# Combined rows gated on VectorE in halves, Silu in the routed experts, scaling behind a split, rows normalized in halves

## The reference

```python
x = L0_attn_x
xn = _layernorm(x)
s = sigmoid attention of xn (q, k layer-normed; scores - log S), projected, * layerscale
g = _silu(_L0_ffn_ref(xn, ...))     # 16 routed experts (top 4) + a shared expert: silu(x @ gate) * (x @ up) @ down
x = x + s * g
xn = _layernorm(x)
s = _L1_attn_ref(xn, k, v)          # a bank of 2048 keys: gelu(scores / norm * sqrt(n)) @ v
g = _silu(_L1_ffn_ref(xn, ...))     # ternary weights: gelu(xn @ W1 + b1) @ W2 + b2
x = x + s * g
```

## Time and profile before

| what | us |
|---|---|
| median of 3 runs (1235.54 to 1235.79) | 1235.58 |
| the profiled execution, time | 1233.56 |
| the profiled execution, span | 1231.8 |
| DVE busy | 875.9 (71%) |
| ACT busy | 553.7 (45%) |
| POOL busy | 423.0 (34%) |
| second attention with its projection | about 525 to 741 |
| routed experts | about 324 to 525 |
| ff stage | about 749 to 890 |

### The profile page before, as it was taken

One profiled execution on the slowest core, in us unless ns is written; L12 is line 12 of the kernel. 1 busy time (PEld: TensorE's weight loads), 2 busy tenths in 40 slices (PEclk: granted clock), 3 DMA queues, 4 the chain that ended last, 5 costly groups with the idle time before them and its releaser, 6 DMA issues.

```text
span 1231.8 us, 26611 instructions
## 1 busy us (share of the span) xinstructions
PE 1195.6 (97%) x8888; PEld 851.7 (69%) x8889; DVE 875.9 (71%) x1893; ACT 553.7 (45%) x1050; POOL 423.0 (34%) x376
## 2 busy tenths in 40 slices
PE   5899999999999999999999999999999999999998
PEld 4556566676688888866666667767766666666665
DVE  8697965556668766678889889998765545555554
ACT  6545632333366666665343345666542222222221
POOL 3353777776036460056777742212000000000000
PEclk8999999999999999999999999999999999999999
DMA  9488355553297665522566647541211011101100
GB/s 300 169 336 319 117 172 167 166 187 134 72 290 229 202 193 188 165 82 76 151 208 196 192 137 241 162 138 37 68 52 52 18 35 52 52 0 51 52 18 18
DMA packets 137830, 169.14 MB, mean 137 GB/s; under 512 B 12899, under 2 KB 126710, under 8 KB 135446
## 3 DMA queue, kind: packets, MB, share of 16 engines
q1 hardware_dynamic: 114438, 125.49, 31.2%
q0 software_dynamic: 12368, 33.70, 8.6%
q10 hardware_dynamic: 10944, 8.92, 2.3%
HBM read 84.18 MB, written 83.89 MB: 136 GB/s over the span
## 4 chain that ended last, share of the span: by engine, by line
PE 75%; DVE 14%; issue 6%; ACT 3%; DVEq 1%; DMA 1%; SPq 0%; ACTq 0%
PE bank L1219 25%; PE sums L1275 15%; PE sums L1234 11%; PE bank L1138 7%; PE sums L1148 4%; PE bank L1080 3%; PE bank L1118 3%; DVE reg_w L2162 2%; DVE stat L1880 2%; PE sums L1090 1%; PE sums L1071 1%; DVE reg_e L2152 1%; DVE reg_qk L1835 1%; DVE reg_w L1835 1%; PE bank L1183 1%
## 5 line engine op out<-in xcount | busy, mean ns | idle before, releaser
L2162 DVE TENSOR_SCALAR reg_w<-reg_w 128x512 f16<-128x512 f32 x320 | 148.4, 464 | 200.3 <-ACT reg_w L1659 199.7
L1835 DVE SCALAR_TENSOR_TENSOR reg_w<-reg_w 128x512 f16<-128x512 f32 x320 | 222.7, 696 | 11.0
L1234 PE MATMUL sums<-reg_v,reg_w 128*128 128x256 f16 x1536 | 188.1, 273 | 1.6 <-DVE reg_w L1835 1.6
L1275 PE MATMUL sums<-reg_v,reg_w 128*128 128x256 f16 x1536 | 188.3, 273 | 0.0
L1219 PE MATMUL bank<-reg_qk,kbT 128*128 128x512 f16 (+1 forms) x768 | 186.7, 379 | 0.0
L1219 PE MATMUL bank<-reg_qk 128*128 (+1 forms) x768 | 186.6, 379 | 0.0
L1659 ACT ACTIVATE reg_w<-bank 128x512 f32<-128x512 f32 x128 | 76.4, 597 | 241.8 <-PE bank L1219 241.8
L1234 PEld LDWEIGHTS sums<-reg_v,reg_w 128*128 128x128 f16 x1536 | 150.0, 98 | 46.3 <-DVE reg_w L1835 3.1
L1275 PEld LDWEIGHTS sums<-reg_v,reg_w 128*128 128x128 f16 x1536 | 150.2, 98 | 44.3
L1659 ACT ACTIVATE reg_w<-bank,nlogs 128x512 f32<-128x512 f32 x128 | 88.0, 688 | 164.7 <-PE bank L1219 158.3
L863 POOL DMA_INDIRECT reg_e<-yg_d,slot_i x128 | 130.9, 1023 | 46.6 <-issue 34.1
(11 more groups left out here) (241 smaller groups left out, 1661.3 us busy)
## 6 DMA issues: line engine op xcount, KB each, us to landing
xg_d<-kbT SPq DMA_DIRECT2D x18, 1024.0 KB, 4.9
xin<-xg_d SPq DMA_DIRECT2D x72, 256.0 KB, 2.8
yg_d<-xr SPq DMA_DIRECT2D x72, 256.0 KB, 2.2
reg_qk<-in_L_attn_x_dram SPq DMA_DIRECT2D x8, 512.0 KB, 7.7
sh_d<-xin SPq DMA_DIRECT2D x16, 256.0 KB, 2.4
xr<-xn_d SPq DMA_DIRECT2D x32, 128.0 KB, 2.6
reg_e<-sh_d SPq DMA_DIRECT2D x32, 128.0 KB, 2.9
moe_d<-reg_e SPq DMA_DIRECT2D x32, 128.0 KB, 1.9
```

Source lines behind the costliest of these rows:

```text
L1234: mm = pe.matmul(sums[:, bass.ds((c & 1) * (2 * 512) + q * D, D)], (ah, al)[x][:, j % 4, q * P:(q + 1) * P], m.second(y, j), start=(j == 0 ...
L1275: mm = pe.matmul(a_bank[2 * i + q // 2][:, (q % 2) * D:(q % 2 + 1) * D], part[:, j % 4, q * P:(q + 1) * P], m.second(y, j), start=(j == 0 ...
L1835: ins = dve.scalar_tensor_tensor(out=out_ap, in0=in_ap, scalar=scale, in1=hi_ap, op0=ALU.mult, op1=ALU.subtract)
L2162: dve.tensor_scalar(ah[:, j % 4, :], att[:, j % 2, :], m.split, None, ALU.mult).then_inc(m.hi_done, 1)
```

## The change

Four edits, on DVE, ACT and POOL:

1. The gated product in the ff stage goes from POOL to DVE, in halves of 128 x 512 behind the splits of j = 0 and 1. The sum onto x moves one step back (j = 1 and 2), all statistics go behind j = 3.
2. ACT normalizes two row groups of chunk c + 2 behind tile 7 of chunk c and the other two behind tile 0 of chunk c + 1. The semaphore for PE is raised after the second half.
3. In the second attention `scale_rows` of chunks 0 to 2 goes behind the split of tile 2 of the next chunk.
4. The routed experts use Silu on ACT; the product at L2064 and its semaphore go. A one-element Silu before and a one-element Sigmoid after the stage bring the table loads to those places.

```diff
@@ gpsimd @@
-            def gated(c):
-                i = c % 2
-                pool.wait_ge(g_ld[i], 32 * (c // 2) + 32)
-                pool.tensor_tensor(gin[i], gin[i], sin[i], ALU.mult).then_inc(q4["m2"], 1)
...
-            pool.wait_ge(q4["l1"], at(1))
-            gated(2)
             for c in range(NCH):
                 if c + 2 < NCH:
                     row_powers(c + 2)
-                if c + 3 < NCH:
-                    gated(c + 3)
                 query_powers(c)
@@ scalar @@
             def sigmoid_gate(expert, c, i):
...
-                act.wait_ge(m["t1"], at(c - 2))
+                act.wait_ge(m["h"], at(c - 2))
...
-                               ACT.Sigmoid, scale=1.0 / QK_PS).then_inc(m["sig"], 1)
+                               ACT.Silu, scale=1.0 / QK_PS).then_inc(m["sig"], 1)
...
+                act.activation(no_rows[:, 0:1], onesf[:, 0:1], ACT.Silu)
                 for c in range(2):
                     rows_hi(c, c % 2)
...
                 rows_out(NSLOT_T // 2 - 1, 3, NSLOT_T // 8 - 1)
+
+                act.activation(no_rows[:, 0:1], onesf[:, 0:1], ACT.Sigmoid)
...
-            def norm_x1(c):
+            def norm_x1(c, halves=(0, 1)):
                 i = c % 2
-                act.wait_ge(q4["nmr"], at(c))
-                act.wait_ge(q4["nn"], at(2 * (c - 3) + 1))
-                act.wait_ge(q4["qs"], at(c - 3))
-                for m in range(G4):
+                if 0 in halves:
+                    act.wait_ge(q4["nmr"], at(c))
+                    act.wait_ge(q4["nn"], at(2 * (c - 3) + 1))
+                    act.wait_ge(q4["qs"], at(c - 3))
+                for m in (m for h in halves for m in (2 * h, 2 * h + 1)):
...
-                ins.then_inc(q4["xn"], 1)
+                if 1 in halves:
+                    ins.then_inc(q4["xn"], 1)
...
             def side(c, j):
-                if j == 0 and c > 1:
-                    queries_hi(c - 2, 1, s_bank[3])
+                if j == 0:
+                    if c > 1:
+                        queries_hi(c - 2, 1, s_bank[3])
+                    if c and c + 1 < NCH:
+                        norm_x1(c + 1, (1,))
...
                 elif j == 7 and c + 2 < NCH:
-                    norm_x1(c + 2)
+                    norm_x1(c + 2, (0,))
@@ vector @@
                 dve.wait_ge(m["sig"], at(c))
-                dve.tensor_tensor(t3, sg[:, i, :].rearrange("p (e c) -> p e c", e=2), ps[:, :, 0:IM], ALU.mult
-                                  ).then_inc(m["t1"], 1)
-                dve.wait_ge(m["t1"], at(c))
                 dve.wait_ge(m["tr"], at(c - 2))
-                dve.scalar_tensor_tensor(out=hh[:, i, :].rearrange("p (e c) -> p e c", e=2), in0=t3,
-                                         scalar=H_S / (QK_PS * QK_PS), in1=ps[:, :, IM:2 * IM],
+                dve.scalar_tensor_tensor(out=hh[:, i, :].rearrange("p (e c) -> p e c", e=2),
+                                         in0=sg[:, i, :].rearrange("p (e c) -> p e c", e=2),
+                                         scalar=H_S / QK_PS, in1=ps[:, :, IM:2 * IM],
                                          op0=ALU.mult, op1=ALU.mult).then_inc(m["h"], 1)
...
                         split(c, j)
+                        if j == 2 and m is at_mix[1] and not first_step(c):
+                            scale_rows(m, c - 1, 1 - i)
...
                 ins.then_inc(m.evac_read, 1)
+                if (m is at_mix[0]) != (isinstance(c, int) and c == m.nch - 1):
+                    scale_rows(m, c, i)
+
+            def scale_rows(m, c, i):
+                rows_ = at_rows[at_mix.index(m)][i]
                 dve.wait_ge(m.evac_read, at(m.ch(c)))
...
+            def gated_half(c, h):
+                i = c % 2
+                dve.wait_ge(g_ld[i], 32 * (c // 2) + 32)
+                rows_ = slice(2 * h, 2 * h + 2)
+                ins = dve.tensor_tensor(gin[i][:, rows_, :], gin[i][:, rows_, :], sin[i][:, rows_, :], ALU.mult)
+                if h:
+                    ins.then_inc(q4["m2"], 1)
...
                 if c + 2 < NCH:
                     if j < 2:
-                        add_up(c + 2, range(2 * j, 2 * j + 2))
-                    if j in (1, 3):
-                        row_stats(c + 2, range(j - 1, j + 1))
+                        gated_half(c + 2, j)
+                    if j in (1, 2):
+                        add_up(c + 2, range(2 * j - 2, 2 * j))
+                    elif j == 3:
+                        row_stats(c + 2)
                     elif j == 4:
                         row_moments2(c + 2)
```

More of the change, by code:

```diff
@@ L146, in build @@
         mhalf = sb("mhalf", [P, G4])
+        no_rows = sb("no_rows", [P, 1])
         thr = sb("thr", [P, 8])
@@ L438, in build @@
         pj = {n: sem(f"pj_{n}") for n in ("mm", "mv", "ve", "rs", "nmr", "qkn", "vhi", "vlo", "tr", "qhi", "qlo")}
-        steps = ("xt", "xh", "xl", "gu", "sig", "t1", "h", "tr", "hi", "lo", "dn", "ev")
+        steps = ("xt", "xh", "xl", "gu", "sig", "h", "tr", "hi", "lo", "dn", "ev")
         shx = {n: sem("shx_" + n) for n in ("gu", "sig", "h", "hi", "lo", "dn", "ev")}
@@ L1828, in _ @@
                   *(pj[n] for n in ("mv", "ve", "nmr", "vlo", "qlo")),
-                  shx["h"], *(rex[n] for n in ("t1", "h", "lo")), rex["xl"], cb_step, cb_done,
+                  shx["h"], *(rex[n] for n in ("h", "lo")), rex["xl"], cb_step, cb_done,
                   *(q4[n] for n in ("x1", "mv", "ve", "nmr", "l1", "nn", "l2")), bk_b2, bk_silu,
@@ L2061, in inner @@
                 ps = s_bank[i][:, :].rearrange("p (e c) -> p e c", e=2)
-                t3 = t1[:, i, :].rearrange("p (e c) -> p e c", e=2)
                 dve.wait_ge(m["sig"], at(c))
-                dve.tensor_tensor(t3, sg[:, i, :].rearrange("p (e c) -> p e c", e=2), ps[:, :, 0:IM], ALU.mult
-                                  ).then_inc(m["t1"], 1)
-                dve.wait_ge(m["t1"], at(c))
                 dve.wait_ge(m["tr"], at(c - 2))
-                dve.scalar_tensor_tensor(out=hh[:, i, :].rearrange("p (e c) -> p e c", e=2), in0=t3,
-                                         scalar=H_S / (QK_PS * QK_PS), in1=ps[:, :, IM:2 * IM],
+                dve.scalar_tensor_tensor(out=hh[:, i, :].rearrange("p (e c) -> p e c", e=2),
+                                         in0=sg[:, i, :].rearrange("p (e c) -> p e c", e=2),
+                                         scalar=H_S / QK_PS, in1=ps[:, :, IM:2 * IM],
                                          op0=ALU.mult, op1=ALU.mult).then_inc(m["h"], 1)
@@ L2129, in routed_experts @@
                 slot_rows_lo(2, 0)
-                scale_rows(at_mix[0], 1)
+                scale_rows(at_mix[0], S // CW - 1, 1)
                 by(dve, NSLOT_T // 2, 4, one_step, head=32)
@@ L2242, in evac_attention @@
                 ins.then_inc(m.evac_read, 1)
+                if (m is at_mix[0]) != (isinstance(c, int) and c == m.nch - 1):
+                    scale_rows(m, c, i)
+            def scale_rows(m, c, i):
+                rows_ = at_rows[at_mix.index(m)][i]
                 dve.wait_ge(m.evac_read, at(m.ch(c)))
-                if m is at_mix[0] and isinstance(c, int) and c == m.nch - 1:
-                    return
-                scale_rows(m, i)
-            def scale_rows(m, i):
-                rows_ = at_rows[at_mix.index(m)][i]
                 for h in range(2):
```

## The result

The kernel with the change takes 1226.62 us (median, 1225.14 to 1227.13) against 1235.68 before in the same call: the ratio is 0.9924 with the interval [0.9907, 0.9941], so it is faster by 0.76%, 9.1 us. 1228.9 was forecast, with a range from 1227.0.

The account below looks back on a forecast made before the run. TensorE, busy 97% of the span, was taken as the bound, so only its remaining waits could be won: 3.7 + 1.9 + 1.1 = 6.7 us, median 1228.9, range 1227.0 to 1232.4.

Parts of the forecast that it names:

- Parts 1 and 2: ff stage: gated product in halves on DVE and normalizing in halves end PE's stalls, 3.7 us; bounds 0.7 and 4.3.
- Part 3: Second attention: scaling behind the split removes three boundary stalls, 0.2 comes back; 1.9 us, bounds 1.0 and 2.1.
- Part 4: Routed experts: Silu removes 72 DVE products, gaining only at two exposed chains; 1.1 us, bounds 0.4 and 1.6.
- Head and tail: Routed experts' start and end: exposed product-transpose chains each shorter by one product, 0.44 us; start scaling also 0.2 earlier.
- Part 5: Two ACT function loads around the routed experts: hidden, 0 us; bounds 0 and 1.5 for one uncovered load.
- The power on POOL: ff stage: a DVE split starting inside POOL's small power might wait 0.7 us; the earlier trace spoke against it.
- A: ff stage keeps most of its stall as DVE's 1.35 us slack is used up; time 1231.5, chance 0.18.
- B: Boundary gains are lost again later and function loads aren't covered; about 0.5 us left, time 1235, chance 0.06.
- C: ff stage: PE's transpose of the next chunk waits for a late second normalization half; 1238 or more, chance 0.04 including D.
- D: The change doesn't do what it says, for instance the function set switches each step; chance within C's 0.04.

Follow-up runs that it names:

- reduce_behind: Kernel after the change plus a DVE maximum over 256 columns (one SBUF operand) behind each routed step's inner product: routed stage 197.86 us, against 198.10 after.
- longer_step: Kernel after the change plus two idle 128x256 DVE products behind the statistics at step 3 of ff chunks 0 to 5: ff 138.48 us, against 137.98 after.
- norm_only: Kernel before with only the row normalizations halved, the gated product left whole on POOL: ratio to before 0.9968, ff 138.02 us against 141.78.
- again_before: Kernel before, unchanged, as a control, on a chip where every kernel takes about 1431 us: ratio 0.9999 [0.9976, 1.0022].

## Why the prediction was right or wrong

- **Parts 1 and 2**, "4 x 0.81 + 0.27 + 0.2 = 3.7 us": 3.80 measured. The sum and the windows held. The chain told for it (product, late shift, late Gelu) is real but isn't the one cause: the normalization in one piece costs 0.27 per chunk without the product, and the product costs PE nothing once the normalization is halved.
- **Part 3**, 1.9 us: 1.88, and the 0.2 that was to come back is 0.27.
- **Part 4**, 1.1 us, is the step that failed: 3.14 measured, outside its bounds of 0.4 to 1.6. Head and tail, 0.64 and 0.44, were right (0.74 and 0.46). Wrong was "In the steady loop PE goes on without waiting for DVE, so these are worth 0". The steps inside a block do go on; at a block start PE waits under the name "issue", with no engine named, and at three of the four it came 2.2 to 2.3 us behind DVE's product in both kernels, so that it moved with the product. That the chain and not DVE's load did it is shown by reduce_behind; what the sequencer does in the 2.2 us stays open. The 2.8 us in four places of L1118 stood in the waits of before and weren't read against the product's time. Worth 1.56 us there, and 0.35 behind the loop.
- **Part 5**, 0: right. Both loads are covered; the second:

```profile
524.43 0.60 ACT L1470 ACTIVATE xr<-sums 128x512 f32<-128x512 f32 x1 [0.61 <-PE sums L1139]
525.05 1.28 ACT L1620 ACT_TABLE_LOAD   x1
526.34 0.20 ACT L1620 ACTIVATE no_rows<-onesf 128x1 f32<-128x1 f32 x1
526.47 0.38 ACT L1470 ACTIVATE reg_v<-sums 128x256 f16<-128x256 f32 x1
```

It starts 0.02 us after the copy, with no drain, so the figure of 2.66 us that the Trainium skill has for a switch ("ScalarE: Activation LUTs", What ACT_TABLE_LOAD costs) isn't seen here: 1.48 us in sum.
- **The power on POOL** doesn't hold up the split inside it (0.43 us), as the earlier trace rows had it and not as the Trainium skill has it ("SBUF — State Buffer", Who interferes with whom); beside POOL's products of 1024 and 2048 columns the trace agrees with that rule.
- **Rivals.** A: DVE had the slack (longer_step). B: of what was won only 0.27 us in the attention is given back. C: no wait for a transpose of xn. D: two table loads, no more.
- **The range.** The best bounds add up to 4.3 + 2.1 + 1.6 = 8.0 us, a time of 1227.6, and the fast end of 1227.0 lay beyond even that. The same sum with part 4 as measured, 3.7 + 1.9 + 3.14 = 8.7 us, gives 1226.8, outside the range: it was short by that one term. The slow bounds add up to 0.7 + 1.0 + 0.4 = 2.1 us, 1233.5, and not to the 1230.5 given for them.

## What to carry to other kernels

"PE waits for nothing" and "PE waits for issue" aren't the same: where a loop jumps back or loads registers, PE was late by when its last semaphore came, and a shorter chain on another engine (0.44 us here) was worth 0.3 to 0.5 us at most such places though it was worth nothing in the steps between. Count these places before a cut is put down as hidden, and try writing such a loop out before making its body longer. Before work is moved between engines, halve the piece that stands in front of the urgent one; here that alone gave the whole gain of the stage.

## What was not expected of the hardware

- A jump back over 24 steps of PE code cost 7.4 us (steps of 7.55 and 5.09 for 2.62), a block start with a jump over 12 steps 1.4 in the kernel before and 0.9 in the one after, at three of four places. With the same code written out straight a block start cost 0.3 to 0.9 in the kernel before and under 0.2 in the one after.
- DVE's 128x256 product from SBUF alone took 4.10 us beside POOL's 128x2048 one, 0.41 otherwise; a reduce of one SBUF operand and a product with a PSUM operand took 0.41 beside the same work. The split, with one SBUF operand, is held all the same (L2167, 2.08 us beside the 128x1024 product in norm_only).
- One chip took 1431 us for every kernel. In the first attention, while POOL worked at its scatters, PE issued a matmul only every 2 to 3.5 us (from 230 to 250 us in again_before). PE's waits from 200 to 340 us in again_before:

```profile
PE sums L1234 <- issue: 59.9, 28, 3.1
```

and its window (us, then busy time and instructions of PE, PEld, DVE, ACT and POOL, PE's granted clock, the DMA share, GB/s):

```profile
207.00:330.00 123.00, 33.41 (x140) 15.06 (x140) 15.49 (x27) 7.84 (x13) 73.96 (x75) 0.55 0.30 103
```

The kernel before has PE busy for 122.49 us of the same window on its own chip. Why is open.
